# Moving the centring and a series factor to ScalarE, and six products from VectorE to GpSimd, in a fused attention, state-space and feed-forward kernel

## What is computed

```
dA = einsum('bld,dn->bldn', delta, A)                 # 384 channels d, 16 states n
dB_u = einsum('bld,bld,bln->bldn', delta, u, B)
dA_cumsum = exp(cumsum of dA from the right, shifted)
xs = cumsum(dB_u * dA_cumsum, axis=1) / (dA_cumsum + 1e-12)
y = einsum('bldn,bln->bld', xs, C) + u * D            # then * silu(res) @ W_out
...
h = h + ffn(layernorm(h)):
  x_norm = rmsnorm(x, g)
  scale = 127.0 / max(max(abs(x_norm)), 1e-5)
  x_q = clip(round(x_norm * scale), -128, 127) / scale
  up, gate = split(x_q @ w_in.T);  y = silu(gate) * up, quantized again, @ w_out.T
```

## Time and profile before

| | |
|---|---|
| median of 3 runs | 583.96 us (583.26 to 584.58) |
| the profiled execution's own time | 586.59 us |
| its span, first to last instruction | 584.8 us |
| mean granted clock of TensorE | 0.831 |
| VectorE (DVE) busy | 459.4 us, 79% |
| TensorE (PE) busy | 403.8 us, 69% |
| GpSimd (POOL) busy | 398.1 us, 68% |
| ScalarE (ACT) busy | 357.2 us, 61% |

### The profile page before, as it was taken

The page is one execution under the profiler, slowest core; times in us unless marked ns, Lnnn a source line. Parts: engine busy times, 40 slices in busy tenths (PEclk is TensorE's granted clock), DMA queues, the critical chain, the costliest instruction groups (busy, mean ns, idle before and its releaser), DMA issues.

```text
span 584.8 us, 5258 instructions
## 1 busy us (share of the span) xinstructions
PE 403.8 (69%) x1498; PEld 217.5 (37%) x1498; DVE 459.4 (79%) x555; ACT 357.2 (61%) x638; POOL 398.1 (68%) x311
## 2 busy tenths in 40 slices
PE   5998997845587494586764847966656776564853
PEld 2336754522233241252332414523323352232523
DVE  1244644248999999988999799899999889999564
ACT  1135352278579683678676556897746676975352
POOL 2035510066679888679997878799879999989401
PEclk9999998778568977795788868978786797988966
DMA  9900000090000044200003331000045200000000
GB/s 310 201 1 1 2 1 1 15 390 29 0 6 1 0 161 161 108 4 0 1 0 108 114 156 54 5 20 1 0 147 207 79 0 21 1 0 1 0 22 20
DMA packets 10269, 34.35 MB, mean 59 GB/s; under 512 B 2064, under 2 KB 4960, under 8 KB 10016
## 3 DMA queue, kind: packets, MB, share of 16 engines
q1 hardware_dynamic: 9840, 33.23, 16.9%
q10 hardware_dynamic: 400, 0.79, 0.4%
HBM read 32.64 MB, written 1.38 MB: 58 GB/s over the span
## 4 chain that ended last, share of the span: by engine, by line
POOL 34%; DVE 18%; issue 14%; PE 7%; ACT 5%; DVEq 0%; POOLq 0%; ACTq 0%
POOL big L458 15%; POOL big L464 11%; DVE PS L1301 7%; PE PS L601 3%; PE PS L809 3%; DVE big L1310 2%; DVE big L1316 2%; ACT PS L994 2%; ACT big L1003 1%; DVE big L1256 1%; POOL big L486 1%; POOL big L436 1%; DVE big L1406 1%; DVE big L1402 1%; POOL big L440 1%
## 5 line engine op out<-in xcount | busy, mean ns | idle before, releaser
L809 PE MATMUL PS<-big,eighth 128*128 128x384 f32 x384 | 189.2, 632 | 119.4 <-POOL big L464 103.7
L458 POOL TENSOR_TENSOR big<-big,bc 128x768 f32<-128x768 f32 x96 | 178.7, 1870 | 0.0
L1301 DVE TENSOR_TENSOR_SCAN PS<-PS,big 128x768 f32<-128x768 f32 x96 | 168.3, 1753 | 6.7 <-ACT PS L994 5.0
L809 PEld LDWEIGHTS PS<-big,eighth 128*128 128x128 f32 x384 | 85.8, 238 | 203.6 <-POOL big L464 130.2
L994 ACT ACTIVATE PS<-big,Aneg 128x384 f32<-128x384 f32 x192 | 103.9, 573 | 93.6 <-DVE big L1316 57.6
L464 POOL TENSOR_TENSOR big<-big,bc 128x768 f32<-128x768 f32 x60 | 108.7, 1811 | 54.0 <-DVE big L1310 53.6
L1003 ACT ACTIVATE big<-big,guard,Ahalf 128x380 f32<-128x380 f32 x192 | 122.2, 690 | 0.0
L1310 DVE SCALAR_TENSOR_TENSOR big<-big,PS 128x768 f32<-128x768 f32 x60 | 56.9, 949 | 5.6 <-DVE PS L1301 0.9
L417 POOL TENSOR_TENSOR big<-bc,cst_sb 96x1536 f32<-96x1536 f32 x8 | 22.0, 2753 | 44.1 <-ACT bc L901 33.1
L601 PE MATMUL PS<-big,w_in_sb 96*128 96x384 f32 x96 | 41.6, 571 | 5.0 <-DVE big L1256 4.4
L601 PE MATMUL PS<-big 128*64 128x34 f32 (+3 forms) x416 | 44.8, 286 | 0.0
(11 more groups left out here) (155 smaller groups left out, 559.6 us busy)
## 6 DMA issues: line engine op xcount, KB each, us to landing
bc<-bc_rows SPq DMA_DIRECT2D x32, 768.0 KB, 4.6
bc<-in_x_cols_dram SPq DMA_DIRECT2D x3, 512.0 KB, 6.6
bc<-in_x_cols_dram SPq DMA_DIRECT2D x1, 1536.0 KB, 9.7
out_dram<-h SPq DMA_DIRECT2D x4, 288.0 KB, 2.7
big<-in_f_in_dram SPq DMA_DIRECT2D x1, 768.0 KB, 12.1
bc<-in_cw_dram ACTq DMA_DIRECT2D x1, 576.0 KB, 5.8
w_in_sb<-in_w_in_dram SPq DMA_DIRECT2D x1, 576.0 KB, 16.8
big<-in_f_out_dram SPq DMA_DIRECT2D x1, 384.0 KB, 13.7
```

The costliest lines, as they stand in the source:

```text
L458: P.tensor_tensor(pair(vR[:, g % VRING]), part(du, q, m).unsqueeze(1).broadcast_to([128, PAIR, QT]), rows_of(g, 0), ALU.mult).then_inc(sem ...
L809: ins = pe.matmul(y_sum, eighth[:, :], vR[:, g % VRING, QT * e:QT * (e + 1)], start=False, stop=True, skip_group_check=True)
L1301: V.tensor_tensor_scan(h_, h_, vR[:, g % VRING], 0.0, ALU.mult, ALU.add).then_inc(sem("scan_done"), 1)
```

## The change

Four edits:

1. `VECTOR_C` becomes a tuple per quarter: in quarter 0 VectorE multiplies by C only at j = 4, in the other quarters at 1, 4 and 6 as before. Steps 1, 6, 9, 14, 17 and 22 thereby go to GpSimd, and their guards write to SBUF.
2. `series_a` becomes a ScalarE activation (Identity, scale -0.5, bias 1). For quarter 0 the first piece stands before the logarithms, the other two behind them.
3. `center` for quarters 0 to 2 becomes four ScalarE activations (Identity, scale -1, bias the mean), so its result has the other sign; the scale of the quantization takes the sign back (-127). It waits for the statistics and stands in ScalarE's queue behind the step's decay and guards.
4. `SCALAR_WORK` gets the entries series_a = 2 and center = 4.

```diff
-VECTOR_C = (1, 4, 6)
+VECTOR_C = ((4,), (1, 4, 6), (1, 4, 6), (1, 4, 6))
...
-                   exps=2, logs=6, quant_in=4, q1_out=2, tanh0=1, tanh1=1, tanh2=1, tanh3=1, square0=1, square1=1,
+                   exps=2, logs=6, series_a=2, center=4, quant_in=4, q1_out=2, tanh0=1, tanh1=1, tanh2=1, tanh3=1, square0=1, square1=1,
...
-            return g % BLOCK in VECTOR_C
+            return g % BLOCK in VECTOR_C[g // QSTEPS]
...
-            def series_a(q, m=slice(0, CT)):
-                P.tensor_scalar(part(du, q, m), part(later, q, m), -0.5, 1.0, ALU.mult, ALU.add).then_inc(sem("half_series"), 1)
...
-            def center(q):
-                if q:
-                    job_here(pool, "q1", q - 1, 1)
-                P.tensor_tensor(xq, h[:, QB * q:QB * (q + 1), :], dmv[:, q, :, 0:1].broadcast_to([L, QB, D]),
-                                ALU.subtract).then_inc(sem("centered"), 1)
...
-                P.tensor_scalar(S[:, 6], S[:, 6], 127.0, 0.0, ALU.mult, ALU.add).then_inc(sem("q1_scale"), 1)
+                P.tensor_scalar(S[:, 6], S[:, 6], -127.0, 0.0, ALU.mult, ALU.add).then_inc(sem("q1_scale"), 1)
...
+            def series_a(q, m=slice(0, CT)):
+                act.wait_ge(sem("tt_ready"), delta_of(q, m if q == 0 else 0))
+                A.activation(part(du, q, m), part(later, q, m), ACT.Identity, bias=1.0, scale=-0.5
+                             ).then_inc(sem("half_series"), 1)
...
+            def center(q):
+
+                act.wait_ge(sem("var_ready"), q + 1)
+                if q:
+                    job_here(act, "q1", q - 1, 1)
+                for b in range(QB):
+                    ins = A.activation(xq[:, b, :], h[:, QB * q + b, :], ACT.Identity, bias=dmv[:, q, b, 0:1], scale=-1.0)
+                ins.then_inc(sem("centered"), 1)
...
+                for q in due("series_a", g):
+                    series_a(q)
+                for q in due("center", g):
+                    if q < LAST:
+                        center(q)
...
+            series_a(0, 0)
             for m in range(CT):
                 logs(0, m)
+            for m in range(1, CT):
+                series_a(0, m)
```

More of the change, by code:

```diff
@@ L537, in beside @@
                     root(q)
-                for q in due("series_a", g):
-                    pool.wait_ge(sem("tt_ready"), delta_of(q, 0))
-                    series_a(q)
                 for q in due("series_b", g):
@@ L555, in beside @@
                     root_in(q)
-                for q in due("center", g):
-                    if q < LAST:
-                        center(q)
                 for q in due("gain_in", g):
@@ L582, in _ @@
             for m in range(CT):
-                pool.wait_ge(sem("tt_ready"), m + 1)
-                series_a(0, m)
                 pool.wait_ge(sem("half_series"), m + 1)
```

## The result

| | before | after |
|---|---|---|
| median | 583.61 us (583.03 to 584.58), with the runs beside the change | 590.31 us (588.04 to 592.11, 4 runs) |
| ratio, 95% interval | | 1.0111 (1.0073 to 1.0149) |
| the profiled execution | 586.59 us, span 584.8 | 590.21 us, span 588.4 |
| mean granted clock of TensorE | 0.831 | 0.831 |

The kernel became 1.1% slower: 6.7 us on the medians, 3.6 between the two profiled executions (that of before lay 3.0 above this median). The forecast was 581.8 and the range ended at 586.6. Both were wrong.

The account below looks back on a forecast made before the run. VectorE was taken to set the pace in quarter 0, one microsecond there costing nearly one. Terms -2.8 - 2.3 + 3.3 - 0.4 = -2.2 took the median 583.96 to 581.8 us, range 578.5 to 586.6.

Parts of the forecast that it names:

- Steps 13 to 23: Quarter 0's later steps: products 14, 17, 22 give 2.6 us, GpSimd contention takes some back; half taken, 1.3 gained.
- quarter 1: Steps 24 to 47: 3.2 us of VectorE waits nearly all go, late decay 35 costs 0.9; gain 2.3, bounds 0.5 and 3.2.
- quarter 2: Steps 48 to 71: a 3.8 us guard stall at step 57, 0.46 given back; loss 3.3, bounds 2 and 5.
- quarter 3: Only centring moves, in step 78; guard pair 80 slips but stays early; 0.4 us gained, bounds 0 and 1.5.
- GpSimd takes quarter 0's gain back: Rival: VectorE's instructions with both inputs in SBUF wait for GpSimd's current instruction; quarter 0 gains nothing, 584.6 us; chance 0.25.
- ScalarE becomes the pacer: Rival: around the logarithms, added ScalarE work exceeds idle time ahead of just-in-time decays; slower kernel, 587.8 us; chance 0.17.
- The head and steps 0 to 12: Kernel start to scan 13: shorter GpSimd head gains 0.4 us; gain to scan 13 is 1.5, limited by TensorE's chain.
- the stall: At step 57 VectorE waits 3.8 us for guard pair 57, slipped behind two table loads on ScalarE.

Follow-up runs that it names:

- the products alone: Only the six quarter 0 products with C given to GpSimd, against the kernel before; series factor and centring stay on GpSimd: 591.06 us, ratio 1.0112.
- the moves alone: The change with quarter 0's products left on VectorE; centring, series factor on ScalarE and the table entries kept: 581.08 us, ratio 0.9926 to before.
- both undone: The change without the six products on GpSimd and without the two table entries; centring and series factor on ScalarE: 577.39 us, ratio 0.9852 to before.
- the PSUM input: The change with quarter 1's softplus total (behind scan 18) reading one input from PSUM, maximum instead of addition: 586.21 us in one run.
- one product back: The change with step 17's product with C left on VectorE, five products on GpSimd: 583.94 us, ratio 0.9979.

## Why the prediction was wrong

**The step that failed** is "Steps 13 to 23": "Between all and nothing I take half: 1.3", with the bounds "0 and 5.7" for quarter 0. At scan 13 the sum was still good: 1.5 forecast, 2.08 measured. From there to scan 24 it was not +1.3 but -4.5 (2.08 early to 2.41 late), and two instructions hold more than that: -1.73 in the select, -3.29 in the total. The larger (-0.71) and a wait of 1.12 at the gate of step 17 add to them, with the three products given up (2.6) on the other side. The rows had been read: the same instruction in 1.34 and in 3.02. But I took the difference as the price of at most one GpSimd instruction, and "nothing" as the worst case.

What the runs show is that such an instruction ends 1.2 us behind the end of a GpSimd product, and that this need not be the product it met: back-to-back products can go ahead of it. The total was passed by two of them in each of the four traces where they followed at once (the change twice, the products alone, the change without the entries), the select by one in four of five. The larger was never passed: in 26 meetings with a row, over all ten traces, it went in after the product it met, and the next took 2.92 to 2.95 us. What decides between the two I didn't find. So the length of GpSimd's uninterrupted rows doesn't fix what such an instruction takes, but it bounds it: rest of the row + 1.2, for each of the instructions with two SBUF inputs that the changed order puts beside a row. The row that the total met has six products, 203.81 to 214.46, and 3.7 us of it were left. The six products lengthen just these rows, so "nothing" was no lower bound. Idle time of GpSimd summed over the stretch (14.6 forecast, 16.1 measured) says nothing about this; where it lies does.

How much of the miss this step is can be added up in the two profiles, measured less forecast: +0.6 up to scan 13, **-5.8** in steps 13 to 23, -1.3 in quarter 1, +2.9 in quarter 2, +0.5 in quarter 3 and -2.7 in the tail. The whole miss is -5.8 too (584.4 forecast, 590.21 measured), but only because the other five happen to cancel; that is luck.

The rival "GpSimd takes quarter 0's gain back" named the mechanism, at 0.25, but let it stop at zero, so its 584.6 was too low as well. The Trainium skill (SBUF — State Buffer, "Who interferes with whom") says that such a VectorE instruction contends with GpSimd's reads and that the order of issue decides who blocks whom; the traces agree on who contends (4.89 us with two inputs from SBUF, 1.36 with one). They also show that order of issue alone does not decide here: the total was there at 210.78, and GpSimd's products that started at 210.89 and 212.66 went before it. The rival "ScalarE becomes the pacer", 587.8, came nearest in size, for another reason; of its places only 0.19 and 0.53 us at decays 33 and 35 showed.

**The head and steps 0 to 12: right.** 0.68 at scan 0 (forecast 0.4). The gate of step 9 came 1.7 earlier, forecast 1.5. TensorE's chain before it is no longer unbroken, since it now waits for step 7's product, ended near 170.2 (forecast 169.7):

```profile
166.01 1.56 PE L793 MATMUL PS<-big,eighth 128*128 128x384 f32 x4 [1.14 <-POOL big L462]
167.50 0.91 PE L585 MATMUL PS<-big,w_dt_sb 48*128 48x384 f32 x2
170.21 2.04 PE L793 MATMUL PS<-big,eighth 128*128 128x384 f32 x4 [1.80 <-POOL big L462]
```

**Quarter 1: right up to scan 38, partly by luck.** 2.3 forecast; between scans 24 and 38 the change gained 2.5, the moves alone 2.4, the change without the entries 3.1, both undone 2.0. Of the change's 2.5, 0.96 are the larger's, 1.91 us instead of 2.87, which the sum didn't have. A centring took 1.49 us on ScalarE instead of 1.85, and the late decay 35 cost 0.53, forecast 0.9 (that working slips: 277.99 + 3 is the decay's start, not its end). Over the whole quarter, to scan 48, the gain is only 1.05, because of steps 43 to 44 below.

**Quarter 2: the stall right, its price too.** 3.8 forecast; 3.30 plus 0.65 at step 55 measured (forecast 0.5 there), a guard slot at 391.50 that I had put at 390.14 with an earlier VectorE. That the entries cause it is shown: it is in every trace with them and in none without. Undersized was what is given back: 3.4 us between scans 58 and 70 instead of 0.46, because the select (1.33 for 3.02) and the total (1.57 for 2.80) meet less of GpSimd's work. It is the failed step once more, with the other sign. From scan 48 to scan 95 this quarter and the next together gained 0.4 where I had a net loss of 2.9.

**Not predicted at all: two stretches of TensorE.** At steps 43 to 44 VectorE waited 2.19 us for a projection where it had waited 0.70 before. The four matmuls ahead of that projection, after and then before:

```profile
325.40 2.77 PE L585 MATMUL PS<-big,w_in_sb 96*128 96x384 f32 x4
```

```profile
325.41 1.46 PE L601 MATMUL PS<-big,w_in_sb 96*128 96x384 f32 x4
```

It is TensorE's granted clock. In the 3 us that start 1 us behind scan 43, it was 0.92 before and 0.50 in the change; TensorE was at 0.50 in both just ahead of that. And the tail grew by 2.7. The busy time in three-us stretches of that tail, after and then before (PE first, clock is the third number from the end):

```profile
546.00:549.00 3.00, 2.61 (x4) 0.99 (x4) 0.00 (x0) 0.48 (x1) 2.39 (x7) 0.60 0.00 0
549.00:552.00 3.00, 2.26 (x8) 1.92 (x8) 0.56 (x1) 2.45 (x4) 0.00 (x0) 0.50 0.00 0
```

```profile
546.00:549.00 3.00, 2.26 (x12) 1.54 (x11) 0.56 (x1) 1.41 (x2) 1.64 (x4) 1.00 0.00 0
549.00:552.00 3.00, 3.00 (x22) 2.98 (x21) 0.64 (x2) 1.53 (x3) 0.00 (x0) 1.00 0.00 0
```

A clock of 0.50 is TensorE at 1.2 GHz, 1.00 at 2.4. Both programs enter the tail's matmuls from a pause of TensorE (1.30 us before, 2.03 after), and one has the lower clock in them, the other not. The traces fall into groups by this. From 6 to 12 us behind scan 95 the clock is 0.51 or 0.52 in both profiles of the change and without the entries, all three with a tail of 46.8; 0.83 with the PSUM input, tail 45.5; and 1.00 in the other six, with tails of 42.9 to 44.1. The tail comes back in the second profile of the change, so it goes with the program rather than with chance. The 1.3 to 1.5 us at steps 43 to 44 go with the clock in the same way: 0.50 there in both profiles of the change, with the moves alone, without the entries and with the PSUM input, 0.91 to 0.96 in the other kernels, which lose next to nothing. What makes one program get the lower clock and its near twin the higher stays open in both places.

**The sum by its parts**, on medians: products alone +6.2, moves alone -3.8, together +6.7 where the parts would give +2.5. The profiles, each against its own scan 0, show where they don't add: at scan 24 +3.15 and -1.20 make +1.95, and the change has +3.09; at scan 95 +3.66 and -3.91 make -0.25, and the change has +1.62; and the tail is 2.7 longer in the change than in either. So some 4.6 us in the profiles, over half of it the tail's, whose clock I can't explain. The failed step turns the sign of the first quarter, and the products alone, without the stall and without the longer tail, are already slower than before; the size of the result includes the clock's two places, some 4 us. About 3 of the 6.7 us on the medians lie in no place of these traces: the profiles are 3.6 apart, since that of before was 3.0 above its median.

## What to carry over

Before work is given to GpSimd because it has idle time, look where that idle time lies: each VectorE instruction with two SBUF inputs should meet a pause, for it waits for the product it meets and can wait through the rest of the row. A gain that is counted from durations of such instructions must be counted from the changed order of both engines. And a table of costs that decides what is issued ahead can hold up more than the moved work costs: here two entries made 4 us of waiting (3.30 and 0.65) out of work that had fitted.

## What the runs showed that I had not expected

- A VectorE instruction of 128x1152 with two SBUF inputs took 1.33 to 4.91 us, with one input in PSUM 1.36 beside an unbroken row on GpSimd. Its end lay 1.21 or 1.22 us behind the end of GpSimd's row for the total in before, after, the products alone and with one product back, and for the select in before and after. GpSimd's products in these meetings took 1.80 to 1.82 us, as elsewhere: VectorE paid all of it. In 27 other meetings over the ten traces (the larger 26 times, the select once) it ended 1.21 or 1.22 us behind a product with another directly behind, and then that other one took 2.92 to 2.95 us: both engines paid.
- VectorE also got in where a GpSimd instruction with one input followed, and then GpSimd paid. In the products alone the select stood at 190.49 beside a product that ended at 191.80, and ended at 193.02, 1.22 later, while the series factor, which took 1.15 at the same place before, took 2.25. Beside the larger of quarter 0 in before, a one-input operation on 96x4 took 1.19 us (199.50), against 0.19 (202.02) in the change. GpSimd's timeline in the products alone:

```profile
190.00 1.80 POOL L458 TENSOR_TENSOR big<-big,bc 128x768 f32<-128x768 f32 x1
191.78 2.25 POOL L433 TENSOR_SCALAR big<-big 128x1152 f32<-128x1152 f32 x1
```

- The scatter differs between near twins: twelve runs of the change without the entries lie within 10 us (eleven within 8.4), six of the version with both undone within 3.3. A single profiled execution can lie 2 to 3 us from its median, so the account above goes by places in the trace and the verdicts by the ratios.
